# Turning the normalised activations of a gated cross-attention and expert kernel: f32 transposes on TensorE, or f16 halves and a transposing DMA

## What is computed

```python
x = x + tanh(g_xattn[0]) * L0_xattn(layernorm(x), ctx, Wq, Wg, bg, Wkv, Wo)
x = x + tanh(g_ffn[0])   * L0_ffn(layernorm(x), proj1, proj1_bias, proj2, proj2_bias)
x = x + tanh(g_xattn[1]) * L1_xattn(layernorm(x), ctx, mask)
x = x + tanh(g_ffn[1])   * L1_ffn(layernorm(x), gate_weight, gate_up_proj, down_proj, ...)
```

## Time and profile before

| what | us |
|---|---|
| median of 3 runs (range) | 1939.32 (1937.81 to 1941.26) |
| the profiled execution | 1941.13 |
| its span, first to last instruction | 1939.3 |
| PE busy | 1900.6 |
| DVE, ACT, POOL busy | 1035.4, 559.7, 280.7 |
| the 1012 f32 transposes of 128x128 (line 844), busy | 150.1 |

### The profile page before, as it was taken

One profiled execution on the slowest core, in us unless ns is written; L12 is line 12 of the kernel. 1 busy time (PEld: TensorE's weight loads), 2 busy tenths in 40 slices (PEclk: granted clock), 3 DMA queues, 4 the chain that ended last, 5 costly groups with the idle time before them and its releaser, 6 DMA issues.

```text
span 1939.3 us, 25583 instructions
## 1 busy us (share of the span) xinstructions
PE 1900.6 (98%) x10102; PEld 962.7 (50%) x10102; DVE 1035.4 (53%) x2260; ACT 559.7 (29%) x873; POOL 280.7 (14%) x277
## 2 busy tenths in 40 slices
PE   6999998999999999999999999999999999999999
PEld 4556555644444444444444444444544444444444
DVE  7688866764545453443535545554555555545422
ACT  3145423422222221112212233232222333333321
POOL 3023211111102010101100011111111111111111
PEclk9999998999999999999999999999999999999999
DMA  6013322220101111110101020101010101000000
GB/s 218 12 42 124 106 89 82 87 98 17 44 28 60 28 64 50 56 55 22 62 1 55 1 71 1 50 1 50 1 50 1 50 1 45 5 11 13 1 22 22
DMA packets 56041, 86.99 MB, mean 45 GB/s; under 512 B 9042, under 2 KB 17362, under 8 KB 55922
## 3 DMA queue, kind: packets, MB, share of 16 engines
q1 hardware_dynamic: 55922, 85.36, 13.8%
HBM read 60.17 MB, written 25.17 MB: 44 GB/s over the span
## 4 chain that ended last, share of the span: by engine, by line
PE 86%; issue 8%; DVE 3%; POOL 1%; DMA 1%; ACT 1%; POOLq 0%; SPq 0%; DVEq 0%
PE bank L835 44%; PE bank L939 16%; PE bank L1033 10%; PE bank L844 5%; PE bank L919 4%; PE bank L885 1%; PE bank L904 1%; POOL arena L802 1%; PE bank L1020 1%; PE bank L968 1%; PE bank L995 0%; DMA x_after_ffn<-arena 0%; PE bank L984 0%; PE bank L983 0%; DMA arena<-x_after_attention 0%
## 5 line engine op out<-in xcount | busy, mean ns | idle before, releaser
L835 PE MATMUL bank<-arena 128*128 128x512 f16 x4608 | 1043.4, 380 | 3.1 <-DVE arena L1286 2.3
L835 PEld LDWEIGHTS bank<-arena 128*128 128x128 f16 x4608 | 451.0, 98 | 522.7 <-issue 5.5
L939 PE MATMUL bank<-arena 128*128 128x512 f16 x1536 | 352.1, 379 | 1.2 <-DVE arena L1469 1.2
L1033 PE MATMUL bank<-arena 128*128 128x512 f16 x1152 | 264.3, 379 | 0.9 <-POOL arena L802 0.9
L1621 DVE SCALAR_TENSOR_TENSOR arena<-bank,arena 128x512 f32<-128x512 f32 x96 | 72.0, 750 | 332.1 <-PE bank L835 332.1
L939 PEld LDWEIGHTS bank<-arena 128*128 128x128 f16 x1536 | 150.1, 98 | 173.9 <-DVE arena L1469 1.7
L1467 DVE TENSOR_SCALAR arena<-arena 128x512 f16<-128x512 f32 x128 | 69.4, 543 | 305.4 <-ACT arena L1134 305.2
L1134 ACT ACTIVATE arena<-bank,arena 128x512 f32<-128x512 f32 x128 | 99.6, 778 | 457.3 <-PE bank L835 454.3
L802 POOL TENSOR_TENSOR arena<-arena 128x512 f16<-128x512 f32 x96 | 111.1, 1157 | 628.7 <-ACT arena L1171 628.7
L844 PE MATMUL bank<-arena 128*128 128x128 f32 x1012 | 150.1, 279 | 26.4 <-DVE arena L1234 14.1
L1033 PEld LDWEIGHTS bank<-arena 128*128 128x128 f16 x1152 | 112.1, 98 | 128.3 <-POOL arena L802 1.4
(11 more groups left out here) (173 smaller groups left out, 1221.9 us busy)
## 6 DMA issues: line engine op xcount, KB each, us to landing
arena<-in_L_ffn_proj SPq DMA_DIRECT2D x48, 256.0 KB, 2.9
x_after_attention<-arena SPq DMA_DIRECT2D x8, 1024.0 KB, 4.7
arena<-x_after_attention SPq DMA_DIRECT2D x8, 1024.0 KB, 5.6
x_after_ffn<-arena SPq DMA_DIRECT2D x8, 1024.0 KB, 4.5
arena<-x_after_ffn SPq DMA_DIRECT2D x8, 1024.0 KB, 6.2
arena<-in_x SPq DMA_DIRECT2D x7, 1024.0 KB, 5.4
out<-arena SPq DMA_DIRECT2D x7, 1024.0 KB, 4.2
arena<-in_L_ffn_down_proj SPq DMA_DIRECT2D x48, 96.0 KB, 2.0
```

Of the source, the lines that this page charges most:

```text
L835: m = e.matmul(bank[b][:, :], wT[l][:, c, tile * P:(tile + 1) * P], y[h][:, c, :], start=n == 0, stop=n == NPASS - 1)
L939: m = e.matmul(bank[t][:, :], hv[h][:, 0, t * P:(t + 1) * P], w2T[l][:, j, :], start=j == 0 and i == 0, stop=j == NH - 1 and i == 2)
L1033: m = e.matmul(bank[t][:, :], hv[h][:, 0, t * P:(t + 1) * P], dnT[l][:, j, :], start=j == 0 and i == 0, stop=j == NR - 1 and i == 2)
```

## The change

A new step `split` t stands in the plan one task after `norm` t. In it ACT copies the normalised f32 tile to f16 (the hi half) and POOL subtracts that from the f32 tile (the lo half); both go side by side into one of four new tiles `ysp`, of 1024 f16 per partition. `turn` t is now one DMA on SP's queue: it reads 128 partitions of 1024 f16 and writes them transposed as 128 x 8 x 128, hi and lo together, to `yT_both`, the same bytes as `yT`. It waits for the split and for `y_free`. Readers wait for the landing of all four DMAs of the layernorm (`y_ready`). PE, ACT and DVE have nothing left to do in `turn`, and it takes no bank. For the A layernorms all four turns stand together at the end of the tasks, and the tasks themselves are taken up somewhat earlier in the plan; the small loads and the load of Wkv and ctx move behind the turns of the first layernorm.

```diff
         def step(t):
-            if t > 1:
-                add("turn", i, t - 2, banks=1)
             if t < NT:
                 add("norm", i, t)
+            if 0 < t <= NT:
+                add("split", i, t - 1)
+            if i[0] != "A" and t > 1:
+                add("turn", i, t - 2)
+            elif i[0] == "A" and t == NT + 1:
+                for k in range(NT):
+                    add("turn", i, k)
...
-        if i == 3:
+        if i == NT + 2:
             add("small")
-        if i == 4:
             add("kvload")
...
-            if 0 < b < NB and j >= 2:
+            if 0 < b < NB:
                 norms.pop(0)()
...
-                if b > 0 and j == 0:
+                if j == 0:
                     for _ in range(2):
                         norms.pop(0)()
...
+    ysp = [at(207 + 2 * i, D, F16) for i in range(NT)]
...
+    def y_ready(w, i):
+
+        for t in range(NT):
+            w.wait_ge(y_in[t], 16 * nth["rs", i])
...
+            elif kind == "turn":
+                _, i, t = step
+                w.wait_ge(y_lo, nth["split", i, t])
+                y_free(w, i)
+                e.dma_start(y_both(i)[:, :, t * P:(t + 1) * P], ysp[t], transpose=True).then_inc(y_in[t], 16)
...
+            elif kind == "split":
+                t = step[2]
+                w.wait_ge(y_hi, n)
+                e.tensor_tensor(ysp[t][:, D:2 * D], yn_s[(n - 1) % 2], ysp[t][:, 0:D], ALU.subtract).then_inc(y_lo)
...
-            if kind == "turn":
-                w.wait_ge(const, C_ID)
-                w.wait_ge(yn_ok, n)
-                turn4(step, yn_s[(n - 1) % 2], y_turned)
-            elif kind == "wturn":
+            if kind == "wturn":
...
-                w.wait_ge(y_lo, y_rank(("A", b)))
+                y_ready(w, ("A", b))
...
+            if kind == "split":
                 _, i, t = step
-                w.wait_ge(y_turned, n)
-                y_free(w, i)
-                e.activation(y_of(i)[0][:, :, t * P:(t + 1) * P], block4(bank_of[step, 0]), ACT.Copy).then_inc(y_hi)
+                w.wait_ge(yn_ok, n)
+                if nth["rs", i] > 1:
+                    w.wait_ge(y_in[t], 16 * (nth["rs", i] - 1))
+                e.activation(ysp[t][:, 0:D], yn_s[(n - 1) % 2], ACT.Copy).then_inc(y_hi)
...
                 if n > 2:
-                    w.wait_ge(y_turned, n - 2)
+                    w.wait_ge(y_lo, n - 2)
```

More of the change, by code:

```diff
@@ L408, in build @@
     yT = [pair(152, NC, TOK), pair(160, NC, TOK)]
+    yT_both = [at(152 + 8 * i, NC * TOK, F16).rearrange("p (k n) -> p k n", k=2 * NC) for i in range(2)]
     aT = yT[1]
@@ L497, in build @@
     bn1, bn2, var_ok, rs_ok, yn_ok = (sem(n) for n in ("bn1", "bn2", "var_ok", "rs_ok", "yn_ok"))
-    y_turned, y_hi, y_lo = sem("y_turned"), sem("y_hi"), sem("y_lo")
+    y_hi, y_lo = sem("y_hi"), sem("y_lo")
+    y_in = [sem(f"y_in{t}") for t in range(NT)]
     w_chain, w_rec, w_mx, w_zero, w_scaled = (sem(n) for n in ("w_chain", "w_rec", "w_mx", "w_zero", "w_scaled"))
@@ L634, in build @@
         w_landed[w] = landed[w % 4]
-    def y_rank(i):
-        return nth["turn", i, NT - 1]
+    def y_ready(w, i):
+        for t in range(NT):
+            w.wait_ge(y_in[t], 16 * nth["rs", i])
     def bcast(v):
@@ L923, in tensor_program @@
                 _, b, j = step
-                w.wait_ge(y_lo, y_rank(("F", b)))
+                y_ready(w, ("F", b))
                 w.wait_ge(w_lo, n_lo["1"])
@@ L1054, in y_free, with y_both @@
             w.wait_ge(sc_mm, b + 1)
-    def y_of(i):
-        return yT[0] if i[0] == "A" else yT[i[1] % 2]
+    def y_both(i):
+        return yT_both[0 if i[0] == "A" else i[1] % 2]
     def scalar_program(e):
@@ L1232, in vector_program @@
                 if n > 2:
-                    w.wait_ge(y_turned, n - 2)
+                    w.wait_ge(y_lo, n - 2)
                 e.tensor_scalar(yn_s[(n - 1) % 2], x[:, t, :], mv[:, t, 0:1], rs[:, t:t + 1], ALU.subtract,
                                 ALU.mult).then_inc(yn_ok)
-            elif kind == "turn":
-                _, i, t = step
-                hi, lo = y_of(i)
-                cols = slice(t * P, (t + 1) * P)
-                w.wait_ge(y_hi, n)
-                y_free(w, i)
-                e.tensor_tensor(lo[:, :, cols], block4(bank_of[step, 0]), hi[:, :, cols], ALU.subtract).then_inc(y_lo)
             elif kind == "wmax":
```

11 lines of the change are left out of this document (5 added, 6 removed).

## The result

| | us |
|---|---|
| before, median of 5 runs beside it (range) | 1938.81 (1937.81 to 1941.26) |
| after, median of 5 runs (range) | 1948.39 (1946.37 to 1949.54) |
| after / before | 1.0047, 95% interval 1.0033 to 1.0062 |
| after, the profiled execution and its span | 1948.39 and 1946.6 |

The change made the kernel 0.47% slower, 9.6 us. 1915 had been predicted; 1948 is inside the range of 1887 to 1995, but on the other side of no change.

The account below looks back on a forecast made before the run. PE, busy 98% of the span, was taken as the bound. Removed turns of -52.8 us and new waits and other terms summed to -24.3, from 1941.1 to 1916.8, or 1915 against the median; 8-in-10 range 1887 to 1995 us.

Parts of the forecast that it names:

- Turns removed: PE's queue: 120 of 128 turns counted at 0.44 us each, -52.8 us; the other eight counted within their places.
- t = 2.0 and L = 4.2: Transposing DMA of 256 KB: each delays the next by t, 2.0 us, and lands L, 4.2 us, after issue.
- Rival (a): The transposing DMA is as quick as a plain one, t = 0.7 and L = 2.9: -43.5 us, 1896 us; chance 0.22.
- Start: First `q` projection: the turns' DMAs are issued from about 17.2 us and the last lands at 27.4: +7.0 us.
- Sequence 1: Its `q`: splits come straight behind POOL's all-reduce and its idle time, turns land at 108.2 us: +7.5 us.
- Sequence 4: Its `q`: POOL's all-reduce and idle time fall between second and third split, turns land near 231 us: +9.0 us.
- Regular transitions: Attention transitions to sequences 2, 3, 5, 7: turns land at 258.9 us, wanted at 260.3: 0, with 1.4 us to spare.
- Sequence 6: PE's 9.9 us wait at a turn goes and PE does other steps, but DVE still waits for POOL: -3.0 us.
- Expert phase 0, sequence 0's tasks +3.0: `router` turns land in time, 0.7 us to spare: 0; only sequence 0 loses 1.5 us each at `scores` and `router`.
- Clock: PE runs slower after the two new waits of 7.5 and 9 us, 2.5 us booked for each: +5.0 us.
- Rival (b): The DMA goes by pieces, t = 4.6 and L = 6.8, with waits at attention transitions and expert phase: 2032 us; chance 0.25.
- Rival (c): The eight 128x128 blocks of one DMA follow each other, each with its own latency: near 2290 us; chance 0.07.

Follow-up runs that it names:

- e7_late_q: Changed kernel with the layernorm tasks in the q loop starting at the third head group again; the two ahead of the first gate stay moved: 1925.19 us.
- e5_unbunch: e1_late with each turn of an attention-phase layernorm issued as soon as its split is done, instead of four in a row: 1915.09 us.
- e9_spare: e2_hybrid with a second, unawaited DMA transpose to an unread tile behind each of 56 turns of the L and M layernorms of sequences 1 to 7: 1900.1 us.
- e2_hybrid: Changed kernel with the A layernorms turned on TensorE as before, tasks and loads at their old places, the others by DMA: 1900.03 us.
- e11_mix: e2_hybrid with the A layernorms of sequences 6 and 7 by DMA too, turns issued singly, and all split subtractions on VectorE: 1897.07 us.
- e6_unbunch_dve: e5_unbunch with the subtraction of the split on VectorE instead of GpSimd: 1908.04 us.
- e1_late: Changed kernel with both moves of the layernorm tasks undone, in the q loop and ahead of the first gate: 1926.17 us.
- e8_double: e2_hybrid with each turn's DMA issued a second time, to the same place, once the first has landed: 1977.07 us.
- e12_q_from_1: Changed kernel with the tasks in the q loop starting one head group later, at the second: 1923.58 us.

## Why the prediction was wrong

The step that failed is one that isn't there. The diff moves the layernorm's tasks two head groups ahead in the q loop and ahead of the first gate, and no term of the sum prices that. The prediction used the earlier tasks where they help (sequence 4, "`rs` two tasks earlier"), and of a late VectorE it said "banks are the cushion, and I book nothing". In the trace of before `stat` had no wait there, so how long the x had been in when it ran was the question to ask; store, load and landing of x take 12.3 us in the changed kernel. Undoing it in the q loop gives back 24.4 of the 47.1 us (e7_late_q), net of three turn waits of 7.7 us that come instead.

The forecast for stage A was +13, so the miss there is 34 us, and these 24.4 are the larger part. Of the other 10, the rows of e7_late_q show where some lie: the 7.7 us at transitions that were booked at 0, the 3 us of sequence 6 that did not come, and a term for the clock that was too small (below), less what the booked waits cost under their terms. That is a reading of one trace, not an experiment. It is luck that stage A of e5_unbunch, +13.5, meets the forecast's sum: it is a kernel with other places for the tasks and the turns, and with waits at transitions that the sum had at 0.

A slip without effect: the fourth `norm` of the expert block stands at 1291.5, not 291.5.

By the prediction's own steps:

- **Turns removed, -52.8.** Right where it can be read: F and E lost 39.8 us for 92 turns of 0.44, that is 40.5. The 28 of stage A can't be told from its waits.
- **t = 2.0 and L = 4.2.** Too slow: SyncE takes 1.23 us, a turn lands after 3.1, and twice as many go through unnoticed (e9_spare). Rival (a) was right on L (2.9); its t of 0.7 was low, as four turns in a row were never issued less than 1.23 us apart. That e2_hybrid and e11_mix reach 1900 and 1897, near its 1896, does not bear it out: they have the attention phase's turns mostly on TensorE.
- **Start, +7.0.** 26.31 against 20.38, +5.9; with the slower work behind it PE is 8.0 us late by 97.82 (89.81 before), ahead of sequence 1's waits.
- **Sequence 1, +7.5.** The first projection starts at 114.64 instead of 100.74; 13.9 later, of which the start made 8.0: +5.9. The size is near and the path only in part the booked one: of 10.4 us of waits 6.56 came by way of VectorE's `norm`, for which the prediction had no term, and 3.89 by the turns.
- **Sequence 4, +9.0.** GpSimd's idle time after its all-reduce is in the trace (7.24 us, had 7.63), and from sequence 3 to sequence 4 e5_unbunch loses 6.6 us and e6_unbunch_dve, without the split there, 0.4. With the 1.8 us of the removed turns added back that is 8.4. Right.
- **Regular transitions, 0.** Right for the change as made (three turn waits, at the booked places). With the tasks late, it fails by 1 to 4 us at three transitions (e1_late), and single turns give back part of that (e5_unbunch).
- **Sequence 6, -3.0.** Did not come. The wait only moved from the turn to the `numden` behind it: 12.3 us, and 9.2 in e7_late_q, against 9.9 before.
- **Expert phase 0, sequence 0's tasks +3.0.** PE waited 0.75 and 0.94 us, once each, and F and E together came out as priced.
- **Clock, +5.0.** Too small. In stage A PE is busy 384.4 us, against 386.2 before; but all 36 turns of the stage are gone (144 matmuls), 15.8 us at 0.44, so the rest of the work ran some 14 us longer (an estimate from these rows), at a granted clock of 0.95 against 0.97 over the stage. In e7_late_q, with fewer short waits, it is 8 us, so about 6 of the 24.4 us are of this kind.
- **Rival (b)**, a slow DMA, was the wrong cause. e8_double shows what it would have been worth in F and E: spacing 4.5 us (b had 4.6) and +79 us, where (b) had booked 40 and a share of the clock's 17. It had 20 for `router` (17.2 measured) and 20 for sequence 0's tasks (21.9), but nothing for `scores` (18.5), and 19 us of slower running.
- **Rival (c)**, with the Trainium skill's 1309 ns for a 128x128 block (VectorE: DVE Perf Modes, the three transpose paths), does not describe this when it is taken once per block: eight blocks in one DMA landed after 3.1 us, 0.39 us a block. The skill's 261 GB/s (DMA: Bandwidth & Descriptors, on latency and other measured facts) gives an estimate of 1.0 us per 256 KB, nearer to the 1.23 us of issue and the 1.4 us of engine time.
- **"No bound by itself"** for GpSimd's subtractions was right for its busy time (429.6 us) and wrong for its place: 7 us, by the late turns of sequence 4 and by VectorE's `norm`, which waits for the split before last. The weight loads behind the turns cost VectorE 7.3 us of waits at L1253; their effect at the end was not tried apart.

From the changed kernel to e2_hybrid stage A falls by 48.6 us: tasks of the q loop 24.4; turns singly 11.0; subtraction off GpSimd 6.2; turned on TensorE with the loads in their old place 8.8; the two tasks ahead of the first gate -1.8, which the medians don't confirm. These are edits laid one on the other, and each is the difference of two single executions. What stays open: the 10 us above; and e12_q_from_1 with single turns and the split on VectorE was not run, and might end a little under e6_unbunch_dve.

## What to carry to other kernels

A step that left PE's queue was gained one for one where nothing else moved and its result came in time (F and E, 39.8 us for 92 turns), and was lost where the same diff moved tasks. So price each moved task by the time at which its input lands, on the engine that takes its steps in order, before pricing the new resource. A transposing DMA in this kernel was cheap (1.23 us of the issuing queue, 3.1 us to landing, 256 KB) and suited layernorms whose reader is many matmuls away; where the reader comes next, TensorE's 0.44 us turn stayed the better one, and the choice can be made per place, as e11_mix does. Turns that each waited for the last one's landing added 3.1 us apiece (e8_double); issued one behind the other without waits they cost nothing (e9_spare).

## What I had not expected of the hardware

- A DMA that turns a 128x1024 f16 tile, spread over 1056 packets, lands 3.1 us after issue (median), as a plain 256 KB load does (3.1 us in the same page). Twice the number of them over the 801 us of stage E changed nothing (DMA share 0.17 to 0.27).
- GpSimd stands 6 us before and 7 us after each partition all-reduce with no releaser (6.18 and 7.24 us in e5_unbunch). The operation itself is 0.38 us; its neighbours pay.
- A DVE wait of 4.0 us did not reach PE, one of 8.2 us did. Waits don't add up: with 16.5 us on x e12_q_from_1 ends where e7_late_q ends with 0.2 us, since it has 6.8 us less of turn waits and about as much more of others.
- With 14 waits of PE of 1.7 to 5.2 us in stage E (856 us) the granted clock was 0.98 instead of 1.00, and the same matmuls took 18.9 us longer: half as much again as the 35.7 us of waits. The traffic was not it: e9_spare has the DMA share and a clock of 1.00.
